# Wider and fewer products of constants ahead of the first attention projection of a two-layer transformer

## The reference

```
x = LN(x + ssm(x))                 # state space mixing, projected by W_o
x = LN(x + experts(x))             # 8 experts, each token to its best 2
x = LN(x + attention(LN(x)))       # 16 heads of 16, own norm with weights ln_w, ln_b
x = LN(x + down(silu(gate) * up))  # inputs and weights quantised in blocks of 16
```

## Time and profile before

| | us |
|---|---|
| median of 3 runs | 1659.35 |
| lowest and highest | 1656.58, 1663.86 |
| the profiled execution | 1659.25 |
| its span | 1657.5 |
| TensorE busy | 1544.3 (93%) |
| VectorE busy | 1306.9 (79%) |
| ScalarE busy | 920.9 (56%) |
| GpSimd busy | 292.2 (18%) |

### The profile page before, as it was taken

The page is one execution under the profiler, slowest core; times in us unless marked ns, Lnnn a source line. Parts: engine busy times, 40 slices in busy tenths (PEclk is TensorE's granted clock), DMA queues, the critical chain, the costliest instruction groups (busy, mean ns, idle before and its releaser), DMA issues.

```text
span 1657.5 us, 29778 instructions
## 1 busy us (share of the span) xinstructions
PE 1544.3 (93%) x11390; PEld 1015.6 (61%) x11390; DVE 1306.9 (79%) x2525; ACT 920.9 (56%) x1407; POOL 292.2 (18%) x395
## 2 busy tenths in 40 slices
PE   5977899999899999899999989999998899999986
PEld 1756889999874333787433378743337775333684
DVE  3585466653459999898999979899998989999595
ACT  1223344444127888444688854568885455888632
POOL 0053222321411120211111112111110210000030
PEclk8999999999899999999999999999999999999998
DMA  3126878777324220002422000232200023220000
GB/s 123 51 77 186 248 245 248 250 252 215 93 39 94 53 43 9 1 1 64 83 52 50 15 1 1 64 76 54 55 15 1 1 49 55 41 40 3 1 1 26
DMA packets 80479, 123.25 MB, mean 74 GB/s; under 512 B 13681, under 2 KB 56082, under 8 KB 80338
## 3 DMA queue, kind: packets, MB, share of 16 engines
q1 hardware_dynamic: 70578, 92.77, 21.5%
q0 software_dynamic: 9760, 28.58, 6.1%
HBM read 76.84 MB, written 18.61 MB: 58 GB/s over the span
## 4 chain that ended last, share of the span: by engine, by line
PE 71%; DVE 20%; issue 3%; ACT 3%; DMA 2%; SPq 1%; POOL 0%; DVEq 0%; POOLq 0%
PE PS L1156 15%; PE PS L1107 13%; PE PS L1016 7%; PE PS L1142 6%; PE PS L1004 6%; DVE MX L1704 6%; PE PS L1274 4%; PE PS L1264 4%; PE PS L955 2%; PE PS L1076 2%; PE PS L1091 2%; PE PS L949 2%; DVE OT L1546 1%; PE PS L1298 1%; PE PS L1226 1%
## 5 line engine op out<-in xcount | busy, mean ns | idle before, releaser
L1704 DVE TENSOR_REDUCE MX<-PS 128x1 f32<-128x512 f32 x1024 | 634.9, 683 | 27.5 <-PE PS L1107 23.6
L798 ACT ACTIVATE Pb<-PS 128x1024 f32<-128x1024 f32 x512 | 519.4, 1025 | 123.0 <-PE PS L1142 120.3
L1107 PE MATMUL PS<-Ks,Qs 48*128 48x512 f32 x1024 | 388.4, 454 | 2.2 <-DVE MX L1704 0.9
L1142 PE MATMUL PS<-Qs,Ks 50*128 50x512 f32 x1024 | 360.6, 452 | 0.0
L1156 PE MATMUL PS<-Pb,V 128*32 128x256 f32 x4096 | 320.5, 390 | 0.5
L1107 PEld LDWEIGHTS PS<-Ks,Qs 48*128 48x128 f32 x1024 | 160.3, 184 | 200.0 <-DVE MX L1704 134.5
L1156 PEld LDWEIGHTS PS<-Pb,V 128*32 128x32 f32 x4096 | 83.8, 108 | 164.4 <-ACT Pb L798 108.7
L1142 PEld LDWEIGHTS PS<-Qs,Ks 50*128 50x128 f32 x1024 | 143.8, 185 | 24.2 <-ACT Pb L798 19.8
L1016 PE MATMUL PS<-Pb,OT 128*128 128x256 f32 x624 | 141.0, 379 | 0.0
L1004 PE MATMUL PS<-Ks,Qs 128*128 128x256 f32 x936 | 126.5, 292 | 11.9 <-DVE Ks L1568 10.5
L1004 PEld LDWEIGHTS PS<-Ks,Qs 128*128 128x128 f32 x936 | 118.6, 195 | 15.1 <-DVE Ks L1568 12.4
(11 more groups left out here) (313 smaller groups left out, 2231.3 us busy)
## 6 DMA issues: line engine op xcount, KB each, us to landing
Pb<-W SPq DMA_DIRECT2D x78, 512.0 KB
y_slot<-V SPq DMA_DIRECT2D x39, 256.0 KB
Qs<-Qh SPq DMA_DIRECT2D x120, 64.0 KB, 2.3
Ks<-Kh SPq DMA_DIRECT2D x120, 64.0 KB, 2.3
V<-b SPq DMA_DIRECT2D x39, 128.0 KB
XT<-x_mid POOLq DMA_DIRECT2D x4, 1024.0 KB
out<-Pb POOLq DMA_DIRECT2D x4, 1024.0 KB, 6.3
OT<-xT SPq DMA_DIRECT2D x2, 1024.0 KB, 6.4
```

What stands on the lines that cost most here:

```text
L798: F["ex"].inc(act.activation(weights_of(n), PS[:, 2 * (n % 2):2 * (n % 2) + 2, :], ACT.Exp, scale=0.25))
L1107: F["slp"].inc(pe.matmul(PS[:, slot_bank(i), :], Qs[rows, p % NB, t * P:(t + 1) * P], Ks[rows, p % NB, kh * HALF:(kh + 1) * HALF], start=T ...
L1142: ins = pe.matmul(PS[:, 2 * (n % 2) + a, :], Ks[rows, p % NB, kt * P:(kt + 1) * P], Qs[rows, p % NB, qh * HALF:(qh + 1) * HALF], start=Tru ...
L1704: F["sld"].inc(dve.tensor_reduce(MX[:, p % 2, a, t, kh:kh + 1], PS[:, slot_bank(i), :], AX.X, ALU.max))
```

## The change

Two calls of `identities` become calls of `warm`. Ahead of the turn stand 32 products of 512 columns in place of 130 of 128 columns, in the same bank 0. Behind the turn stand 3 of 512 columns in place of 8 of 128, in the same bank 7. All other calls of both helpers stay, and no wait and no operation of another engine changes.

```diff
@@ -1042,7 +1042,7 @@
                     ins = pe.matmul(PS[:, 1, j:j + 1], wqkv[:, kc, j * P:(j + 1) * P], lnb[:, kc:kc + 1],
                                     start=(kc == 0), stop=(kc == DC - 1))
             C["wb"].inc(ins)
-            identities(130, 0)
+            warm(32, 0)
             C["one"].wait(pe, 16 * 2 * 2)
 
             def turn(b, ahead):
@@ -1308,7 +1308,7 @@
                         qk_unit(b, 1, u)
 
             turn(0, 0)
-            identities(8, 7)
+            warm(3, 7)
             C["ql"].wait(pe, 1)
             F["xtl"].wait(pe, 0, 4)
             for u in range(4):
```

## The result

The changed kernel took 1648.91 us (median of 6 runs, 1645.74 to 1655.17), the kernel before beside it 1658.9 (6 runs, 1656.58 to 1663.86). The ratio is 0.9942 with a 95% interval of 0.9918 to 0.9965, about 10 us less. The forecast was 1651.2 us. The profiled execution of the changed kernel took 1652.04 us with a span of 1650.3.

A forecast was written before the change was run, and what follows sets the result against it. TensorE's constants ahead of the turn held up the kernel for about 10 us; eighth turn at 456.25 plus 4.15 puts the projection at 460.4 instead of 468.48, so 1659.25 − 8.1 = 1651.2 us, range 1647 to 1660.5.

The forecast's parts named there:

- The chain and what is late next: From turn to projections: ScalarE's rows (L740) pace the turn, then the wide products behind it end last, projection at 460.4 us.
- The term of the first edit: Ahead of the turn: 64 wide records, 0.43 us each, end at 450.3 us, before the first row at 452.67 us.
- The term of the second edit: Behind the turn: 3 wide products take 2.58 us where 8 narrow took 1.79, a cost of 0.79 us.
- The gap ahead of the turn: TensorE waits 2.4 us before the first row; a low clock spell could cost 0 to 1.7 us, taken as 0.
- Rival 4: Constants ahead of the turn: ordinary executions lack the profiled slow issue, so the change costs 0.8 us, 1660.1 us; chance 0.10.
- Rival 3: Slow issue belongs to a place in the code, returns in the projections at about 465 us, 1662.0 us; chance 0.08.
- Rival 1: Ahead of the turn: slow issue comes from the gathers alone, stays at its time; +0.1 us, up to 1653.5; chance 0.10.

The follow-up runs named there:

- first edit alone: Against the kernel before, 32 wide products replace the 130 narrow ones ahead of the turn, the 8 narrow ones behind it stay; 1646.84 us, ratio 0.9982.
- changed kernel with its code moved: Changed kernel plus 38 narrow products (152 instructions) some 390 us earlier, in TensorE's wait ahead of L949; 1644.12 us in one run.
- the moved code: Kernel before plus 38 narrow products (152 instructions) some 390 us earlier, in a wait of TensorE; 1654.61 us in one run.
- wide and narrow kernel: Against the kernel before, 16 wide and then 65 narrow products replace the 130 narrow ones ahead of the turn; 1651.10 us in one run.

## Why the prediction was right

*The chain and what is late next* held. The first row released the turn, the eighth turn began 4.10 us behind L740's start (4.17 were worked out), and the projections followed when the last wide products ended, as forecast.

*The term of the first edit* was right in mechanism and size: 0.43 us a record, no pause, TensorE there when the row arrives. Worked out were 8.1 us for both edits, and the distance fell by 8.1. Medians fell by 10, with an interval of 5.8 to 13.6 us (0.35 to 0.82% of 1658.9) that holds the 8.1; the 1.9 us on top are not in the place.

*The term of the second edit*: 0.79 us worked out, 8.6 − 7.8 = 0.8 measured between the changed kernel and the first edit alone.

*The gap ahead of the turn.* I took its price as 0, with a bound of 1.7 us. In the first trace the gap was only 0.42 us, because the low spell lay ahead of it and ate it. In the second it was 2.04 us and cost 0.7 us. But the first edit alone waited 2.56 us in the same gap and the changed kernel with its code moved 2.16 us, and both kept the clock at 1.00 through the turn. So the bound was sound, the value of 0 holds for two of the three executions with such a gap, and the one that had the spell had the shortest wait of the three; the likeness to 1.89 us of idle time in a stretch of 10 was a poor reason.

*Rival 4* is where the reasoning failed, though it didn't decide this result. I had given it only 0.10 because the profiled time lay 0.1 us from the median of three runs. That shows only that the executions of one measurement are alike. In two other measurements with 40 runs the kernel before took 1649.4 and 1649.8 us, none of the traces taken there shows the slow issue, and there the change gave 0.9986 (0.9972 to 1.0000; measured in the second of the two). That the forecast of the gain came true is to this extent luck: it was worked out from a trace with the slow issue, and the changed kernel was measured on the same occasion. The rival's price, 0.8 us to the bad, is what the place shows there; the medians are 2.6 us the other way. The first edit alone is 2.5 us below the kernel before (0.9982, 0.9970 to 0.9994) with an equal distance in the place, and the kernel without constants ahead has a distance 2.6 us longer and a median 1.1 us lower (ratio 0.9998, 0.9985 to 1.0010). So 2 to 4 us come from somewhere the traces don't show. In single traces the part behind the projections varies by more than that (1184 to 1189 us over the runs), so it stays open.

*Rival 3*, one place in the code, fell with the moved code. *Rival 1*, the gathers alone, would have had the wide products slowed; they weren't, in either trace of a measurement in which narrow ones were. What I gave as two separate causes, pace and gathers, seem to act together; but in the wide kernels no fetch of code fell among the gathers either, so it isn't shown that the pace alone spared them.

## What to carry to other kernels

Products of constants that only keep TensorE at work aren't always free if they are many instructions: for the same microseconds use the widest product, since on the occasions with the slow issue the wide ones ran through and the narrow ones cost 8.9 us. Ask too what they are worth: here, 1.1 to 1.8 us. Read which input they cover, and size them to end with it; behind the turn three wide products were 0.8 us longer than eight narrow ones and ended behind the input they cover, so the first edit alone is the better kernel by the place. And before a stall in one trace is taken for the kernel's own, run the kernel again on another occasion: three equal runs of one measurement are one observation.

## What the runs showed of the hardware

Of kernels with much the same code, on the same chip, some executions have a stretch in which TensorE issues only one instruction each 0.35 to 0.75 us for 3.8 to 10.8 us with nothing to wait for, and others don't (in the wide and narrow kernel one record and its load took 1.43 us, from 443.01 to 444.44, where at full pace they take 0.11). By the times of the kernel before it comes and goes from one measurement to another and is alike within one. And keeping the clock up over 27 us was worth 1.1 to 1.8 us: with TensorE idle for 29 us the clock stood at 0.50 until 464.6 us, and the turn ran at 0.64 us a step, TensorE's own pace at that clock, in place of ScalarE's 0.49; the projections had the full clock again.
